# The judging stage's first layer: node parts multiplied once per node instead of once per edge

## The reference, cut to what matters

```python
N, E, HID, OUT = 12500, 400000, 64, 32      # the sizes of this input
e_feat = jnp.concatenate([x[rol], x[col], edge_attr], axis=-1)   # source, destination, attributes: 96 numbers
h = jax.nn.relu(e_feat @ W1 + b1)            # W1 is 96 x 64
v = h @ W2 + b2                              # W2 is 64 x 32
x_cand = jax.ops.segment_max(v, col, num_segments=num_nodes)
return jnp.maximum(x_cand, x[:, -v.shape[-1]:])
```

## Time and profile before

| what | value |
|---|---|
| median of 3 runs | 14325.05 us (14324.3 to 14400.83) |
| profiled execution | 14359.44 us, span 14357.7 us |
| busy: PE, DVE, ACT, POOL | 8012.0, 7383.5, 4852.9, 8443.8 us |
| attention stage's gathers (L652) | first at 351.7, last at 5278.9 us |
| scatters (L1245) | first at 7485.8, last at 7608.3 us |
| judging's gathers (L1352) | first at 7623.1, last at 12172.5 us |
| next stage's gathers (L1560) | first at 12225.7 us |
| memory traffic | 139 GB/s over the span |

### The profile page before, as it was taken

One profiled execution on the slowest core, in us unless ns is written; L12 is line 12 of the kernel. 1 busy time (PEld: TensorE's weight loads), 2 busy tenths in 40 slices (PEclk: granted clock), 3 DMA queues, 4 the chain that ended last, 5 costly groups with the idle time before them and its releaser, 6 DMA issues. The chain is left out here.

```text
span 14357.7 us, 254566 instructions
## 1 busy us (share of the span) xinstructions
PE 8012.0 (56%) x99382; PEld 6554.0 (46%) x99382; DVE 7383.5 (51%) x8080; ACT 4852.9 (34%) x7120; POOL 8443.8 (59%) x7325
## 2 busy tenths in 40 slices
PE   2555555555555545988862344444444434488987
PEld 2444444444444434988861111111111111488987
DVE  4666666666666656666751222222222222666666
ACT  1444444444444433655540000000000000355655
POOL 5777777777777771313136666666666666331313
PEclk7555555555555557999986666666666666799999
DMA  5222223232323225989871222222222222598988
GB/s 92 82 85 89 86 87 89 86 90 86 89 84 90 89 71 202 350 318 332 331 245 41 55 54 58 57 58 55 56 56 56 58 53 58 189 328 319 351 305 285
DMA packets 1047494, 1997.20 MB, mean 139 GB/s; under 512 B 327105, under 2 KB 645527, under 8 KB 1047311
## 3 DMA queue, kind: packets, MB, share of 16 engines
q1 hardware_dynamic: 587603, 1664.35, 31.4%
q0 software_dynamic: 235776, 185.47, 8.3%
q10 hardware_dynamic: 224060, 146.71, 4.1%
HBM read 1617.67 MB, written 381.43 MB: 139 GB/s over the span
## 5 line engine op out<-in xcount | busy, mean ns | idle before, releaser
L652 POOL DMA_INDIRECT attend_and_count_rows<-table,attend_and_count_ring x3136 | 3927.9, 1253 | 1076.4 <-issue 1001.2
L1352 POOL DMA_INDIRECT judge_edges_src_rows<-table,judge_edges_ring x3136 | 3023.8, 964 | 1536.6 <-issue 955.9
L1201 POOL DMA_INDIRECT base<-slot_sums,last_slot x588 | 995.2, 1693 | 2977.8 <-DMA slot_sums<-propagate_mean_whole 1406.8
L687 PE MATMUL attend_and_count_counts<-attend_and_count_hot_hi,attend_and_count_hot_lo 128*128 128x98 bf16 x15680 | 1442.0, 270 | 2321.8 <-ACT attend_and_count_stage L796 1420.2
L687 PEld LDWEIGHTS attend_and_count_counts<-attend_and_count_hot_hi,attend_and_count_hot_lo 128*128 128x128 bf16 x15680 | 1191.7, 133 | 2571.2 <-ACT attend_and_count_stage L796 1400.6
L796 ACT CAST attend_and_count_stage<-attend_and_count_counts 128x784 uint8<-128x784 f32 x1960 | 1531.8, 812 | 897.5 <-PE attend_and_count_counts L687 536.3
L1108 PE MATMUL propagate_mean_p_dense<-propagate_mean_split,propagate_mean_part 128*128 128x96 bf16 x36456 | 1662.0, 208 | 303.4 <-ACT propagate_mean_part L1005 233.2
L1108 PE MATMUL propagate_norm_p_dense<-propagate_norm_split,propagate_norm_part 128*128 128x96 bf16 x36456 | 1663.2, 208 | 243.3 <-ACT propagate_norm_part L1005 169.1
L1108 PEld LDWEIGHTS propagate_mean_p_dense<-propagate_mean_split,propagate_mean_part 128*128 128x128 f16 x36456 | 1638.5, 100 | 311.2 <-ACT propagate_mean_part L1005 233.3
L1108 PEld LDWEIGHTS propagate_norm_p_dense<-propagate_norm_split,propagate_norm_part 128*128 128x128 f16 x36456 | 1641.4, 100 | 251.2 <-ACT propagate_norm_part L1005 170.0
L1489 ACT ACTIVATE judge_edges_hidden<-judge_edges_p_hid,judge_edges_b 128x512 f32<-128x512 f32 x392 | 247.7, 685 | 4236.8 <-remote 3145.4
(11 more groups left out here) (262 smaller groups left out, 12025.1 us busy)
## 6 DMA issues: line engine op xcount, KB each, us to landing
propagate_mean_raw<-matrix SPq DMA_DIRECT2D x372, 1568.0 KB, 8.8
propagate_norm_raw<-matrix SPq DMA_DIRECT2D x372, 1568.0 KB, 8.8
matrix<-attend_and_count_stage SPq DMA_DIRECT2D x245, 784.0 KB
scan<-attend_and_count_out SPq DMA_DIRECT2D x196, 272.0 KB
inject<-attend_and_count_zeros SPq DMA_DIRECT2D x49, 1024.0 KB
attend_and_count_rows<-table,attend_and_count_ring POOLq DMA_INDIRECT x3136
judge_edges_src_rows<-table,judge_edges_ring POOLq DMA_INDIRECT x3136
judge_edges_dst_rows<-inject SPq DMA_DIRECT2D x195, 256.0 KB
```

The costliest lines, as they stand in the source:

```text
L652: nc.gpsimd.indirect_dma_start(out=rows[:, u, g, j, :], out_offset=None, in_=D.table0[:, :], in_offset=rows_of(ring[:, u, g, j:j + 1])).th ...
L687: last = nc.tensor.matmul(counts[:, r % 2, k // 4, NH * (k % 4):NH * (k % 4) + NH], hot_lo[:, u, slot, :], hot_hi[:, u, slot, :], start=Tr ...
L1201: nc.gpsimd.indirect_dma_start(out=sums[:, h, :], out_offset=None, in_=D.slot_sums[0:blocks * BLOCK, :], in_offset=rows_of(S.last_slot[:, ...
L1352: nc.gpsimd.indirect_dma_start(out=src_rows[:, u, lane, :], out_offset=None, in_=D.table2[:, :], in_offset=rows_of(ring[:, u, lane:lane + ...
```

## The change

Three things move together.

1. `spread_nodes` multiplies each node's features by the source part and by the destination part of W1. Four tiles of nodes at a time are transposed on PE (L1253 of the new kernel), copied out by ACT, multiplied by a block-diagonal weight (L1264) and copied to SBUF by DVE (L1273). The results, 64 numbers for each part, go to two tables, `table2` and `table2_dst`, and the destination part is what POOL scatters into `inject`. Each scatter now waits for its batch. The tables are stored when all 25 batches are made.
2. `judge_edges` gathers and loads rows of 64 numbers (256 B) in place of 32. `lift` keeps only the attributes' product, 2 products a step instead of 6, and waits only for the attributes. DVE transposes destination and source rows in two halves each, scans two halves, and a new `join` of step n-1 adds both to the product in PSUM (2 sums of 1,024 columns). The transposed destination rows lie in PSUM now. ACT's `rectify` waits for `join` instead of `lift`.
3. `inject` is twice as wide, so its zeroing in the attention stage writes 2 MB a turn instead of 1 MB; the semaphores of the first stages are freed after them, with one more barrier of all engines.

The diff, cut (lines that only rename buffers or halve indices are left out):

```diff
@@ attend_and_count: the zeros that become inject
-                             .rearrange("(p t r) f -> p t (r f)", p=P, t=ATTEND_STEPS),
-                             zeros[:].unsqueeze(1).to_broadcast([P, ATTEND_STEPS, EACH * FEAT])).then_inc(inject_zeroed, 16)
+                             .rearrange("(p t r) f -> p t (r f)", p=P, t=2 * ATTEND_STEPS),
+                             zeros[:].unsqueeze(1).to_broadcast([P, 2 * ATTEND_STEPS, EACH * FEAT])).then_inc(inject_zeroed, 16)
@@ spread_nodes
+    TILES_AT_ONCE = 4
+    BATCHES = [slice(h, min(h + TILES_AT_ONCE, NH)) for h in range(0, NH, TILES_AT_ONCE)]
+    ends = sb("ends", [P, NH, 2, HID], f32)
...
         def _(sp):
-            sp.dma_start(D.table2[:, :].rearrange("(h p) f -> p h f", p=P), S.x[:]).then_inc(stored, 16)
+            sp.wait_ge(blank, 1)
+            for t in range(TILES_AT_ONCE):
+                for part in range(2):
+                    sp.dma_start(w_ends[t * FEAT:(t + 1) * FEAT, t, part], D.W1[part * FEAT:(part + 1) * FEAT, :]).then_inc(w_loaded, 16)
...
+            sp.wait_ge(made, len(BATCHES))
+            for part, table in enumerate((D.table2, D.table2_dst)):
+                sp.dma_start(table[:, :].rearrange("(h p) f -> p h f", p=P), ends[:, :, part]).then_inc(stored, 16)
+            sp.wait_ge(stored, 32)
...
+        @block.tensor
+        def _(pe):
+            def turn(n, tiles):
+                if n >= 2:
+                    pe.wait_ge(kept, n - 1)
+                wide = (tiles.stop - tiles.start) * FEAT
+                nc.tensor.transpose(p_xt[0:wide, n % 2, 0:P], S.x[:, tiles].rearrange("p h f -> p (h f)"), S.ident[:]).then_inc(turned, 1)
...
+                nc.tensor.matmul(p_ends[:, n % 2, 0:many * 2 * HID], xt[0:many * FEAT, n % 2],
+                                 w_ends[0:many * FEAT, 0:many].rearrange("k t w f -> k (t w f)"), start=True, stop=True).then_inc(multiplied, 1)
...
+                nc.vector.tensor_copy(ends[:, tiles].rearrange("p t w f -> p (t w f)"), p_ends[:, n % 2, 0:many * 2 * HID]).then_inc(made, 1)
...
             for h in range(NH):
+                pool.wait_ge(made, h // TILES_AT_ONCE + 1)
                 nc.gpsimd.indirect_dma_start(out=D.inject[:, :], out_offset=rows_of(S.first_edge[:, h:h + 1]),
-                                             in_=S.x[:, h, :], in_offset=None).then_inc(placed, 16)
+                                             in_=ends[:, h, 1, :], in_offset=None).then_inc(placed, 16)
@@ judge_edges
-    src_rows = sb("src_rows2", [P, RING, ROWS, FEAT], f32)
-    dst_rows = sb("dst_rows2", [P, RING, ROWS, FEAT], f32)
+    src_rows = sb("src_rows2", [P, RING, ROWS, HID], f32)
+    dst_rows = sb("dst_rows2", [P, RING, ROWS, HID], f32)
...
+    p_firsts = pb("p_firsts", [P, HALVES, CHUNK], f32)
...
                 pe.wait_ge(edges_turned, here + 1)
-                pe.wait_ge(held, here + 1)
-                pe.wait_ge(src_turned, here + 1)
                 for half in range(HALVES):
-                    for part, feat in ((2, attr_feat), (1, dst_feat), (0, src_feat)):
-                        last = nc.tensor.matmul(p_hid[:, u % 2, half], w1[:, part, half], feat[:, u % 2],
-                                                start=(part == 2), stop=(part == 0))
+                    last = nc.tensor.matmul(p_hid[:, u % 2, half], w1[:, half], attr_feat[:, u % 2], start=True, stop=True)
...
-                nc.vector.transpose(by_lane(firsts[:]), dst_rows[:, u]).then_inc(spaced, 1)
+                for half in range(HALVES):
+                    await_count(dve, held, here * HALVES + (half - 1))
+                    last = nc.vector.transpose(by_lane(p_firsts[:, half]), dst_rows[:, u, :, half * FEAT:(half + 1) * FEAT])
+                last.then_inc(spaced, 1)
...
+            def join(it, u):
+                here = it * RING + u
+                dve.wait_ge(lifted, here + 1)
+                dve.wait_ge(held, here * HALVES + HALVES)
+                nc.vector.tensor_tensor(p_hid[:, u % 2], p_hid[:, u % 2], dst_feat[:, u % 2], ALU.add).then_inc(joined, 1)
+                dve.wait_ge(joined, here * 2 + 1)
+                dve.wait_ge(src_turned, here + 1)
+                nc.vector.tensor_tensor(p_hid[:, u % 2], p_hid[:, u % 2], src_feat[:, u % 2], ALU.add).then_inc(joined, 1)
...
                 front(it, u)
+                if not (isinstance(it, int) and it + u == 0):
+                    join(*before(it, u, 1))
                 if not (isinstance(it, int) and it * RING + u < 2):
                     top(*before(it, u, 2))
...
-                act.wait_ge(lifted, here + 1)
+                act.wait_ge(joined, here * 2 + 2)
@@ graph_layers
-    D.inject = dram("inject", [E_PAD + N_PAD, FEAT], f32)
+    D.inject = dram("inject", [E_PAD + N_PAD, HID], f32)
...
-    D.table2 = dram("table2", [N_PAD, FEAT], f32)
+    D.table2 = dram("table2", [N_PAD, HID], f32)
+    D.table2_dst = dram("table2_dst", [N_PAD, HID], f32)
...
+            nc.clear_and_free_semaphores(early)
+            nc.all_engine_barrier()
```

83 lines of the change are left out of this document (58 added, 25 removed).

## The result

| | median | runs | lowest to highest |
|---|---|---|---|
| before | 14349.99 us | 20 | 14307.23 to 14400.83 |
| changed | 14299.51 us | 20 | 14234.94 to 14339.48 |

The ratio is 0.9962, 95% interval [0.9951, 0.9973]: 50 us faster, within 1%, so no change by the bound of the prediction. The forecast was 13831 us, the range 13700 to 14190; the result lies outside of both. The profiled execution of the changed kernel has a span of 14326.7 us, against 14357.7.

The account below looks back on a forecast made before the run. POOL was taken to pace judging, stopped about every third step by a late source list behind PE's late signals. -614 + 80 + 10 + 25 + 5 = -494 us on 14359.4 gave 13865, 34 less for the median: 13831 us; range 13700 to 14190.

Parts of the forecast that it names:

- POOL's floor: Judging: 3,136 gathers at 0.944 + 0.311 us plus 53 us make 3989 us, 614 under the 4602.6 of before.
- Scan against gather: Judging: a DVE scan of two SBUF operands lengthens gathers; reading rows from PSUM saves 63 us, included in the floor.
- PE's signals and its records: Judging: PE's signals lag as if each record took 1.4 us; 16 records fewer leave 22.4 us a step.
- DVE costs nothing with POOL as cover: Judging: DVE grows from 6.61 to 12.4 us a step (13.1 at most), under POOL's 20.1, so costs nothing.
- The new wait: Judging: join makes DVE wait for PE's lift signal, but lags may reach about 46 us before POOL starves, formerly 22.
- what is left of the stops: Judging: POOL still stops 20 or fewer times, 12 us each, at most 240 us; 80 taken.
- Rival B: Judging: join makes DVE wait on a late signal, 700 us slower, 15,060 us; chance 0.06.
- Memory: Judging: rows of 256 B add 2 x 256 KB a step; nothing to a few us a step, nothing taken.
- Zero fill: Attention stage: 49 DMAs grow by 1 MB, 240 us if POOL waited each time; 10 taken.
- spreading and barrier: Spreading: work before the first scatter and batches feeding the scatters cost 25 us; the extra barrier 5.
- C: Judging: PE's signal lag goes altogether, stage 3989 us, kernel 13750 us; chance 0.22.
- A: Judging: the lag belongs to the signal, not the records; four fifths of 570 us of stops stay, 14190 us; chance 0.12.

Follow-up runs that it names:

- x5: Changed kernel, loading rows and flags of the first four steps only, both products and all DVE operations of judging on 64 of 512 columns; judging 4402.4 us.
- x6: x5 with the stores of the maxima moved behind the last gather; 22.27 us a step.
- x9: x5 with gathers of 64 rows in place of 128; 22.35 us a step.
- z2: x5 with gathers of 8 rows in place of 128, on a fifth chip; 22.37 us a step.
- e1: Kernel before with the source's and destination's products left out of the lift; judging 4507.2 us.
- e4: Changed kernel without the two sums of the join; judging 4507.3 us.
- x10: x5 with gathers of 8 rows in place of 128, on another chip; judging 3649.2 us, 18.54 us a step.
- x12: Kernel before with the source's product alone left out of the lift; judging 3978.7 us.
- y4: Changed kernel with ACT loading the edges' rows three steps ahead, after its rectify; 13497.49 us, ratio 1.0017 to the kernel before on that chip.
- e2: Changed kernel with gathers of 32 numbers in place of 64, used for both halves; judging 4526.3 us.
- e3: Kernel before with rows of 64 numbers gathered, 32 of them used; judging 4598.9 us.
- x4: Changed kernel with all of DVE's operations of judging on 64 of 512 columns, same count; judging 4512.3 us.
- x1: Changed kernel with rows and flags of the first four steps only loaded; judging 4405.9 us.
- x7: Changed kernel with 60 register instructions meant on GpSimd ahead of each step's gathers; 22.90 us a step.
- x8: x5 with 60 register instructions meant on GpSimd ahead of each step's gathers; 22.31 us a step.

## Why the prediction was wrong, by its own steps

- *POOL's floor (-614).* **The step that failed.** "3,136 gathers x (0.944 + 0.311)" took the pace of gathers in a kernel that stops every third step as the pace of gathers that never stop. The sustained gather is 1.395 us by itself on the three chips where that was run (x5; x6 and x9; z2) and 1.431 with the loads beside it: 3136 x 1.431 + 31 = 4518 us, measured 4517.3, where the 1.431 is of the same trace. On the chip of e1 to e4 only kernels with loads ran, at 1.43. On the chip of x10, x12 and y4 it is 1.248 (y4), and the floor of 3989 was right within 51 us; but there the kernel before seems to have no such stops to lose. Its judging there is 3900 to 3970 us, an estimate from its 13482 us and the other stages of x12 and y4, since no trace of it was kept on that chip. Its 13482 us against y4's 13497 say that the forecast would have been wrong there too, for another reason.
- *Could the rows have warned?* Not of the rate. A step of the kernel before is 23.23 us in the mean, of which the stops are 2.9; against 22.3 only 0.9 of these could be had, 0.3 with the loads. But its first two turns of four steps, without stops, took 81.2 and 81.5 us, 1.27 us a gather, as the floor has it, and no longer stretch without stops was in judging. The one such stretch of the kernel is the attention stage, 4927 us for 3,136 gathers, 1.57 each. I took the median of its gathers as a price, where their mean is 1.25 us, and left its pace out of the range. The prediction did name the sign, "gathers or their spacing longer than 1.255 us", and gave it no chance and no price.
- *Wider rows cost nothing.* Right: e2 and e3.
- *Scan against gather (63).* Right in kind, unseen in the sum, since the rate covers it. Without the rate it shows: x12, which keeps the scan of two SBUF operands, has a mean of 957 ns, y4 943: 14 ns x 3,136 = 44 us. In x12 142 of the 389 gathers beside that scan are over 1 us, and none apart from it is over 0.962; in y4 541 lie beside a scan that reads PSUM, and none is longer than 0.962. The rule of the Trainium skill, "SBUF — State Buffer", section "Who interferes with whom", holds in these two traces.
- *PE's signals and its records.* Right in effect: 24 to 8 records in a lift took the stops away, alone (e1). The cause stays half open. The lag of 1.4 us for a record looks like a mark of the condition, not a property of TensorE: in x12 there is none. That the same 1.40 us stands between two gathers and between SyncE's instructions is a likeness that I didn't follow up.
- *DVE costs nothing with POOL as cover.* Right: 11.8 us a step (12.4 forecast; its upper bound adds up to 12.7, not 13.1), and x4, with a quarter of it, is no faster.
- *The new wait; what is left of the stops (80).* No stops at all, and DVE waits 1381.5 us for gathered rows, POOL never for DVE. Rival B had no ground.
- *Memory (nothing).* Under the rate, loads cost 0.58 us a step (22.90 against 22.33 in x1), 114 us. y4, without it, has 20.0 us a step with all loads. How much of it the wider destination rows add was not tried alone; e1, with the old loads, has 22.83.
- *Zero fill (10), spreading and barrier (30).* Attention stage 7 us shorter where 10 longer was forecast, spreading 36 us longer: near enough.
- *The rivals.* C had the mechanism, stops gone altogether, and the same wrong floor. None held a second limit right under the first. A, with stops kept and 14190 us, came nearest and for the wrong reason.

The sum as it came: -85 + 36 and 18 us of other stages in the profiled pair, -31 us; the medians differ by 50.

## What to carry to other kernels

An idle time in front of the engine that sets the pace is worth its length only if the engine can keep its pace without it. Ask for a long stretch without stops and divide its length by the count; a median of single instructions, taken from a stretch with pauses, doesn't tell. Where the kernel has no such stretch, make one: e1, one line of the kernel before, would have shown the second limit ahead of the change. When a large expected gain vanishes and the busy time of the same instruction grew by that much, look for a second limit right beneath the one removed, and take everything away from around the instruction: one kernel (x5) ended the theories about its neighbours. Read in the trace that an edit did what it was meant to (x7 and x8 have no pause). And run on more than one chip before a cause is named.

## What the runs showed of the hardware

- On three chips GpSimd's gathers fall from 1.16 to 1.25 us to 1.40 us each (with their gap) after 100 to 164 of them without a pause, whether they have 8, 64 or 128 rows and with next to nothing beside them; the reserve is 16 to 18 gathers. With the rows' loads beside them it is 1.44 us, on these chips and a fourth. On one more chip, that of y4, 3,136 in a row ran at 1.25 us.
- Where that holds, SyncE's register moves in the changed kernel's judging take 0.70 us instead of 0.04, and in the kernel before ACT starts 35.5 us after the matmul records that it waits for. The attention stage is the same on all chips (4915 to 4938 us). From its last gather to judging's first it is 2335 to 2415 us elsewhere, 2226 to 2272 on the chip of y4.
- What the condition is stays open. The Trainium skill, "DMA: Bandwidth & Descriptors", section "SWDGE vs HWDGE vs iDMA", says that GpSimd writes a pair of descriptors for each DMA operation into rings which the DMA engines drain. These traces show no queue of transfers (2.2 us from a gather's start to its end in x5), but how full the rings are they don't show. The Trainium skill, "NOTIFIC — the notification-queue block", section "Constraints, capacities, measured rates", puts the block's inner store at about 500 records of what the engines report, and its section "Overflow: three behaviours, one of which stalls the engine" says that the block holds the engines back rather than lose a record inside. A rate for each gather with a reserve would look like that. Against it: the attention stage leaves 12.9 records of instructions and 64 of DMA packets per us and shows nothing of the condition, the changed kernel's judging 3.5 and 45. Every run here was recorded in the same way, so none can tell whether the recording slows the engines or something else on those chips does.
